# Control products ahead of a transpose fill, whole squares and a shorter affine in a gated channel sparsifier

## The chip, the cores and the metric

The kernel runs on one core of one Trainium2 chip. The metric is the device time of one execution in microseconds (us). The engines are PE (TensorE; its weight loads are shown as PEld), DVE (VectorE), ACT (ScalarE), POOL (GpSimd) and SP (SyncE, which only issues transfers here).

## What is computed

```python
# x: (32, 512, 56, 56) f32, W1, W3: (512, 512) f32
g = group_norm(x, groups=32, eps=1e-5)           # 16 channels a group
r = relu(g)
r = where(max_hw(r) - mean_hw(r) < 0.5, 0, r)    # per image and channel
bb = 1 - exp(-abs(max_c(r) - mean_c(r)))         # per image and pixel
y = bb * r
x_max, pooled = max_hw(y), mean_hw(y)
control1 = sigmoid(pooled @ W1.T)
control3 = relu(pooled @ W3.T); control3 = where(control3 < 1, 1.2, control3)
out = x + where(y < control1 * control3 * x_max, 0, y)
```

## The kernel before, in words

An image is four tiles (`t` = 0 to 3) of 128 channels x 3136 pixels, f32. Three images of x are kept in `xs`. Tiles 0 and 1 are worked on in place, tiles 2 and 3 in `rs`, so that their x is still there when POOL adds it back; x for tiles 0 and 1 is added by a transfer that accumulates (L787).

Each engine has one program written out by hand; the engines meet only at semaphores, and an engine's instructions run strictly in their order. One turn of the loop over images `s` on each engine holds work for three images: the end of image s-1, the middle of s and the start of s+1.

**ACT.** For image s+1 it squares every tile and sums along the pixels (`square_half`, L437 to L442, two halves of 1568 pixels a tile, written to `junk`, which nobody reads; L441 is the instruction). Each squaring waits until the one before it has been counted by `junk_step`. Between them stand, in the order of L513 to L522: the copy of the control rows of image s-1 out of PSUM (`copy_control`, L494) behind the first half of tile 2, the exponential for the sigmoid (`control_exp`, L498) behind the second half, the copy of the mean rows of image s (`copy_mean_rows`, L470) behind tile 0, that of the means (`copy_means`, L474) behind tile 1. The load order is tiles 2, 0, 1, 3. Then come the row means (`row_means`, L451 and L454), the first gate values (`gate_values`, L479 to L483: absolute value, exponential, 1 minus), the copy of the group's sums (`copy_group`, L459), and the four relus of image s+1 (L465, which applies the group norm as scale and bias), with gate values 1, 2, 3 between them, and then the pool sums of image s (`pool_sum`, L490): three for each tile, of 1536, 768 and 832 pixels, eleven of the twelve after the last relu.

**PE.** In the order of L396 to L428: transposes of image s (`turn`, L288, two blocks of 128 pixels of all four tiles, into one of two PSUM buffers; `turn` i waits until DVE has read buffer i-2), turns 0, 1, 2; the control products of image s-1 (`control_products`, L366: for each tile k, once its last pool sum is there, two matmuls of three columns x 512, in column groups 0 and 32 for even k, 64 and 96 for odd k); the control logits (L374); the mean rows of s (L298, 28 matmuls in four column groups); the sums over x of image s+1, two tiles (`sum_x`, L337); `turn_means` (L306); the other two tiles' sums; turns 3 and 4; the group's matmuls (`group_stats`, L348 for the means, L351 for the squares); `spread` 0 (L318, which puts the gate values into PSUM rows); turns 5 to 8, and so on with the other spreads. `keep_clock` (L325) issues matmuls that nobody reads.

**DVE.** The maxima over channels (`block_max`, L640, one for each turn), the differences (`differ`, L650), the gating with its maximum (`gate`, L657), and for image s-1, behind `block_max` 2, the control (L667 to L684) and the comparison with the threshold (`keep_tile`, L688). `differ` 0 stands between the third and fourth `keep_tile` and waits for the means from ACT.

**POOL.** For image s-1 the accumulating transfers of tiles 0 and 1 (L787), then the affine of image s+1 (`affine`, six small operations, L769 to L779), then the four additions of x for tiles 2 and 3 (L796). The relu of tile 3 waits for the last of these additions.

**SP.** Issues loads (L222) and stores (L232).

Of the kernel before, what the change touches and what calls it, by code (L numbers as in the profile page):

```python
# [4 lines left out]

F32 = mybir.dt.float32
BF16 = mybir.dt.bfloat16
I32 = mybir.dt.int32
ALU = mybir.AluOpType
ACT = mybir.ActivationFunctionType  # L10
# [2 lines left out]
P = 128  # L13
# [32 lines left out]
def gated_sparsifier(nc, x, w1, w3, out):  # L46
# [15 lines left out]
    GMAX = max(GPIX[g + 1] - GPIX[g] for g in range(NG))  # L62
    SUMS = ((0, 2), (2, 3), (3, 4))
    NS = len(SUMS)
    assert T == 4 and NBLK == 25 and LAST_W == 64 and NX * XCHUNK == HW and NM == 7 and GMAX == 832

    x_tiles = x.rearrange("b (t p) h w -> b p t (h w)", p=P)
# [2 lines left out]
    with ExitStack() as ctx:  # L70
        def sb(name, shape, dt=F32):
            return ctx.enter_context(nc.sbuf_tensor(name, shape, dt))
# [7 lines left out]
        xs = sb("xs", [P, XR, T, HW])  # L80
        rs = sb("rs", [P, 2, len(KEPT_X), HW])
        wt = sb("wt", [P, 2, T, C])
        junk = sb("junk", [P, HALF], BF16)
        rows = sb("rows", [P, C])
        control_sb = rows[:, :]
        mean_rows = rows[:, 0:MEAN_ROW]
# [9 lines left out]
        row_part = sb("row_part", [P, 2])  # L96
        ones = sb("ones", [P, 1])
        half_neg = sb("half_neg", [P, T])
        squares = sb("squares", [P, 2, T])
        row_sum = sb("row_sum", [P, 1])  # L100
        row_mean = sb("row_mean", [P, T])
        gst = sb("gst", [P, 2, T])
# [1 line left out]
        gvar = sb("gvar", [P, T])  # L104
        geps = sb("geps", [P, T])
        rstd = sb("rstd", [P, T])
        mrs = sb("mrs", [P, T])
        shift = sb("shift", [P, T])
        rsum = sb("rsum", [P, T])
        peak = sb("peak", [P, T])  # L110
# [91 lines left out]
        def half(tile, h):  # L202
            return tile[:, HALF * h:HALF * (h + 1)]
# [76 lines left out]
        def _(pe):  # L280
# [63 lines left out]
            def group_stats(s):  # L344
                pe.wait_ge(row_mean_ready, s + 1)
                if s > 1:
                    pe.wait_ge(logits_ready, s - 1)
                pe.matmul(ps_group[:, 0, :], group_pick[:, :], row_mean[:, :], start=True, stop=True)  # L348
                pe.wait_ge(squared, 2 * T * (s + 1))
                for h in range(2):  # L350
                    mm = pe.matmul(ps_group[:, 1, :], group_avg[:, :], squares[:, h, :], start=(h == 0),  # L351
                                   stop=(h == 1), skip_group_check=True)
                mm.then_inc(group_sums, 1)

            def count_fails(s):
# [2 lines left out]
                    mm = pe.matmul(ps_count, fails[:, t:t + 1], ones[:, :], start=(t == 0), stop=(t == T - 1))  # L358
                mm.then_inc(count_ready, 1)

            def control_products(s):
                for k in range(T):
                    pe.wait_ge(pooled_ready, NS * T * s + T * (NS - 1) + k + 1)
                    for m in range(2):
                        first = 32 * (m + 2 * (k % 2))
                        mm = pe.matmul(ps_control_rows[first:first + NS, :], pooled[:, k, :], wt[:, m, k, :],  # L366
                                       start=(k < 2), stop=(k >= T - 2), skip_group_check=True,
                                       tile_position=(0, first))
                mm.then_inc(control_rows, 1)

            def control_logits(s):
                pe.wait_ge(control_copied, s + 1)
# [22 lines left out]
            for s in range(B):  # L395
                pe.wait_ge(r_final, s + 1)  # L396
                turn(s, 0)
                turn(s, 1)
                turn(s, 2)
                if s > 0:  # L400
                    control_products(s - 1)
                    control_logits(s - 1)
                mean_rows_of(s)
                if s + 1 < B:
                    sum_x(s + 1, range(0, 2))
                turn_means(s)
                if s + 1 < B:
                    sum_x(s + 1, range(2, T))
                turn(s, 3)
                turn(s, 4)  # L410
                if s + 1 < B:
                    group_stats(s + 1)
                spread(s, 0)
                turn(s, 5)
                turn(s, 6)
                turn(s, 7)
                turn(s, 8)
                spread(s, 1)
                turn(s, 9)
                turn(s, 10)  # L420
                turn(s, 11)
                turn(s, 12)
                spread(s, 2)
                keep_clock(s, 3)
                spread(s, 3)
                if s + 1 < B:
                    count_fails(s + 1)
                    keep_clock(s, 2)  # L428
            control_products(B - 1)
            control_logits(B - 1)  # L430

        @block.scalar
        def _(act):
            steps = Steps(act, act_step)
            junk_step = Steps(act, squared)

            def square_half(s, n, h):  # L437
                t = LOAD_ORDER[n]
                act.wait_ge(x_loaded[s % XR][t][h], 16 * (s // XR + 1))
                junk_step.wait()  # L440
                junk_step.step(act.activation(junk[:, :], half(x_tile(s, t), h), ACT.Square,  # L441
                                              scale=float(HW) ** -0.5, accum_out=squares[:, h, t:t + 1]))  # L442

            def square_tile(s, n):
                for h in range(2):
                    square_half(s, n, h)

            def row_means(s):
                act.wait_ge(sx_summed, s + 1)
                junk_step.wait()  # L450
                steps.step(act.activation(junk[:, 0:XCHUNK], ps_rowsum, ACT.Identity,  # L451
                                          scale=1.0 / (PER_GROUP * HW), accum_out=row_sum[:, :]))
                steps.wait()
                act.activation(row_mean[:, :], row_tile[:, :], ACT.Identity, scale=row_sum[:, :]  # L454
                               ).then_inc(row_mean_ready, 1)
# [42 lines left out]
                act.activation(exp_neg[:, :], logits[:, 0:T], ACT.Exp, scale=-1.0).then_inc(exp_neg_ready, 1)  # L498

            act.wait_ge(consts_ready, 1)  # L500
            for n in range(T):
                square_tile(0, n)
            row_means(0)
            copy_group(0)
# [4 lines left out]
            for s in range(B):  # L509
                has_next = s + 1 < B  # L510
                if has_next:
                    square_half(s + 1, 0, 0)
                if s > 0:  # L513
                    copy_control(s - 1)
                if has_next:
                    square_half(s + 1, 0, 1)
                if s > 0:
                    control_exp(s - 1)
                if has_next:
                    square_tile(s + 1, 1)  # L520
                copy_mean_rows(s)
                if has_next:  # L522
                    square_tile(s + 1, 2)
                copy_means(s)
                if has_next:
                    square_tile(s + 1, 3)
                    row_means(s + 1)
                gate_values(s, 0)
                if has_next:
# [228 lines left out]
        def _(pool):  # L758
# [8 lines left out]
            def affine(s):  # L767
                pool.wait_ge(group_copied, s + 1)
                steps.step(pool.tensor_tensor(gsq[:, :], gst[:, 0, :], gst[:, 0, :], ALU.mult))  # L769
                steps.wait()  # L770
                steps.step(pool.tensor_tensor(gvar[:, :], gst[:, 1, :], gsq[:, :], ALU.subtract))
                steps.wait()
                steps.step(pool.tensor_scalar(geps[:, :], gvar[:, :], 0.0, GN_EPS, ALU.max, ALU.add))
                steps.wait()
                steps.step(pool.tensor_tensor(rstd[:, :], geps[:, :], half_neg[:, :], ALU.pow))  # L775
                steps.wait()
                steps.step(pool.tensor_tensor(mrs[:, :], gst[:, 0, :], rstd[:, :], ALU.mult))
                steps.wait()
                pool.tensor_scalar(shift[:, :], mrs[:, :], -1.0, 1.0, ALU.mult, ALU.mult).then_inc(affine_ready, 1)  # L779

            affine(0)
            for s in range(B):
# [35 lines left out]
```

## Time and profile before

| | |
|---|---|
| median of three runs | 1678.03 us (1676.78 to 1678.05) |
| the profiled execution: its time, its span | 1675.8 us, 1674.0 us |
| busy share | DVE 87%, PE 82%, ACT 81%, PEld 52%, POOL 36% |
| mean granted clock of PE | 0.942 of 2.4 GHz |
| DMA | 309 GB/s in the mean |

The span is the time from the first to the last instruction in the trace; the execution's own time is 1.8 us more, and the median of the runs 2.2 us above that. A busy share is an average over 32 images and tells how close an engine is to being full. It doesn't tell which waits set the time; for that stands the chain, which is followed back from the last instruction to what released it, step by step.

### The profile page before, as it was taken

The page shows a single profiled execution, that of the slowest core. Times are in us where ns is not written, and L with a number is a line of the kernel's source. Part 1 is how long each engine was busy: PE and PEld are TensorE (multiplying, and loading weights), DVE is VectorE, ACT ScalarE, POOL GpSimd, SP SyncE. Part 2 cuts the span into 40 slices and gives each one's busy share as a digit, 9 for nine tenths or more (in the row PEclk, how much of TensorE's full clock was granted, in tenths as well). Part 3 has the DMA queues.
Part 4 walks back from the last instruction along what each step waited for, and adds up shares of the span by engine and source line. Part 5 has one row for each costly group of instructions (what it writes and reads, how often), then busy time and mean ns, then how long its engine had stood idle before and what let it go on. Part 6 is the DMA issues. An engine that isn't in the chain of part 4 may idle for free.

```text
span 1674.0 us, 26770 instructions
## 1 busy us (share of the span) xinstructions
PE 1369.8 (82%) x10204; PEld 866.5 (52%) x10204; DVE 1459.4 (87%) x2192; ACT 1354.3 (81%) x2177; POOL 610.1 (36%) x446
## 2 busy tenths in 40 slices
PE   3889888888888988888888888888888888888761
PEld 1655455555455655455555555555545555545540
DVE  2598889988889988888998888988888998888996
ACT  7788888888888888888888888888888888888821
POOL 0042334442244443244443234443233444234440
PEclk8999999999999999999999999999999999999995
DMA  9259999999999999999999999999999999999973
GB/s 393 119 142 313 344 355 310 310 312 305 344 348 327 307 314 304 334 343 339 308 309 309 325 344 351 306 304 313 317 344 356 308 308 311 307 343 351 308 231 153
DMA packets 93348, 517.69 MB, mean 309 GB/s; under 512 B 10272, under 2 KB 10272, under 8 KB 93216
## 3 DMA queue, kind: packets, MB, share of 16 engines
q1 hardware_dynamic: 75360, 416.38, 61.7%
q0 software_dynamic: 17856, 99.56, 30.4%
q8 instruction: 81, 1.33, 0.3%
q14 instruction: 51, 0.42, 0.1%
HBM read 310.38 MB, written 205.52 MB: 308 GB/s over the span
## 4 chain that ended last, share of the span: by engine, by line
ACT 31%; PE 31%; POOL 29%; DVE 5%; issue 2%; DMA 1%; SPq 0%; DVEq 0%; ACTq 0%
POOL xs L796 25%; PE ps_gate L337 11%; ACT rs L490 11%; PE ps_gate L298 10%; ACT xs L490 9%; ACT rs L465 6%; PE ps_turn L288 4%; ACT junk L441 3%; PE ps_gate L374 2%; POOL rstd L775 2%; PE ps_gate L306 2%; DVE max_and_mean L640 1%; ACT rows L494 1%; PE ps_gate L351 1%; DMA xs<-in_x 1%
## 5 line engine op out<-in xcount | busy, mean ns | idle before, releaser
L640 DVE TENSOR_REDUCE max_and_mean<-ps_turn 128x2 f32<-128x1024 f32 x384 | 463.0, 1219 | 24.5 <-PE ps_turn L288 19.4
L288 PE MATMUL ps_turn<-ident,xs 128*128 128x128 f32 (+1 forms) x1600 | 329.5, 289 | 142.7 <-DVE max_and_mean L640 139.0
L796 POOL TENSOR_TENSOR xs<-xs,rs 128x1568 f32<-128x1568 f32 x124 | 433.3, 3528 | 0.9 <-DVE rs L688 0.9
L787 POOL DMA_DIRECT2D xs<-in_x x124 | 111.3, 966 | 877.9 <-DVE xs L688 780.8
L441 ACT ACTIVATE junk<-xs 128x1568 bf16<-128x1568 f32 x256 | 385.3, 1505 | 9.9 <-ACT junk L441 0.4
L288 PE MATMUL ps_turn<-ident,rs 128*128 128x128 f32 (+1 forms) x1600 | 315.9, 280 | 0.0
L288 PEld LDWEIGHTS ps_turn<-ident,xs 128*128 128x128 f32 (+1 forms) x1600 | 191.4, 144 | 239.5 <-DVE max_and_mean L640 184.5
L318 PE MATMUL ps_gate<-ident,bb 128*128 128x128 f32 (+1 forms) x1600 | 235.6, 301 | 62.4 <-ACT bb L483 61.5
L318 PEld LDWEIGHTS ps_gate<-ident,bb 128*128 128x128 f32 (+1 forms) x1600 | 215.3, 210 | 99.1 <-DVE ymax_parts L657 87.7
L465 ACT ACTIVATE xs<-xs,shift,rstd 128x3136 f32<-128x3136 f32 x64 | 192.1, 3001 | 85.8 <-POOL shift L779 80.5
L657 DVE CUSTOM_DVE_ANT_0 xs<-xs,ps_gate 128x768 f32<-128x768 f32 (+1 forms) x256 | 243.3, 959 | 10.4 <-PE ps_gate L318 8.6
L657 DVE CUSTOM_DVE_ANT_0 rs<-rs,ps_gate 128x768 f32<-128x768 f32 (+1 forms) x256 | 241.0, 961 | 7.5 <-issue 7.5
L465 ACT ACTIVATE rs<-xs,shift,rstd 128x3136 f32<-128x3136 f32 x64 | 192.1, 3002 | 60.5 <-POOL xs L796 60.5
L688 DVE SCALAR_TENSOR_TENSOR rs<-rs,thres 128x3136 f32<-128x3136 f32 x64 | 222.3, 3478 | 0.0
L688 DVE SCALAR_TENSOR_TENSOR xs<-xs,thres 128x3136 f32<-128x3136 f32 x64 | 220.3, 3483 | 1.1
L337 PE MATMUL ps_gate<-xs,sel 128*32 128x448 f32 x1792 | 205.9, 544 | 12.0 <-DMA xs<-in_x 12.0
L288 PEld LDWEIGHTS ps_turn<-ident,rs 128*128 128x128 f32 (+1 forms) x1600 | 206.3, 144 | 1.1
L490 ACT ACTIVATE xs<-xs 128x1536 f32<-128x1536 f32 (+2 forms) x192 | 203.2, 1059 | 1.2 <-DVE ymax_parts L657 1.2
L490 ACT ACTIVATE rs<-rs 128x1536 f32<-128x1536 f32 (+2 forms) x192 | 203.0, 1058 | 0.0
L325 PE MATMUL ps_turn<-wt,ident 128*128 128x512 f32 x316 | 171.5, 678 | 0.6
L337 PEld LDWEIGHTS ps_gate<-xs,sel 128*32 128x32 f32 x1792 | 62.7, 110 | 110.2 <-issue 109.6
L298 PE MATMUL ps_gate<-xs,chan_avg 128*32 128x512 f32 (+1 forms) x896 | 115.9, 542 | 0.0
(82 smaller groups left out, 1158.0 us busy)
## 6 DMA issues: line engine op xcount, KB each, us to landing
xs<-in_x SPq DMA_DIRECT2D x260, 784.0 KB, 13.8
out<-xs SPq DMA_DIRECT2D x256, 784.0 KB, 8.4
xs<-in_x POOLq DMA_DIRECT2D x124, 784.0 KB, 11.0
rs<-in_L_conv_W SPq DMA_DIRECT2D x2, 1024.0 KB, 17.2
```

The source lines that it names most:

```text
L288: mm = pe.transpose(ps_turn[0:w, n % 2, b - 2 * i, P * t:P * (t + 1)], r_tile(s, t)[:, P * b:P * b + w], ident[:, :])
L298: mm = pe.matmul(ps_mean_rows[32 * k:32 * k + 32, 0:w], chan_avg[:, 31 - j:63 - j], r_tile(s, t)[:, MEAN_ROW * j:MEAN_ROW * j + w], start= ...
L318: mm = pe.matmul(ps_gate[:, g % 2, first:first + w], bb[0:w, b:b + 1].to_broadcast([w, P]), ident[0:w, 0:w], start=True, stop=True)
L325: pe.matmul(ps_turn[:, NT * (s + 1) % 2, 0, :], ident[:, :], wt[:, 0, 0, :], start=True, stop=True, skip_group_check=True)
L337: mm = pe.matmul(ps_rowsum[32 * k:32 * k + 32, :], sel[:, t, :], x_tile(s, t)[:, XCHUNK * c:XCHUNK * (c + 1)], start=(q < 4), stop=(q >= N ...
L441: junk_step.step(act.activation(junk[:, :], half(x_tile(s, t), h), ACT.Square, scale=float(HW) ** -0.5, accum_out=squares[:, h, t:t + 1]))
L465: act.activation(r_tile(s, t), x_tile(s, t), ACT.Relu, bias=shift[:, t:t + 1], scale=rstd[:, t:t + 1], accum_out=rsum[:, t:t + 1]).then_in ...
L490: act.activation(y, y, ACT.Identity, accum_out=pooled[:, t, j:j + 1]).then_inc(pooled_ready, 1)
L640: ins = dve.tensor_reduce(max_and_mean[:, 2 * i:2 * i + 2, 0], ps_turn[:, n % 2, :, :], AX.X, ALU.max)
L657: dve.tensor_tensor_reduce(out=y, in0=y, in1=ps_gate[:, g % 2, 0:n], scale=1.0, scalar=0.0, op0=ALU.mult, op1=ALU.max, accum_out=ymax_part ...
L688: dve.scalar_tensor_tensor(r, r, thres[:, t:t + 1], r, ALU.is_ge, ALU.mult).then_inc(kept, 1)
L796: pool.tensor_tensor(o, o, half(r_tile(s - 1, t), h), ALU.add).then_inc(added, 1)
```

## The change

In words: on PE, `control_products` takes the tiles as an argument, and those of tiles 0 and 1 are issued ahead of turn 2, those of tiles 2 and 3 behind it; `group_stats` stands ahead of turn 4 and has three matmuls for the squares instead of two, two of them of one column. On ACT, the first tile to be squared is done in pieces of 784, 784 and 1568 pixels, every other tile in one instruction of 3136; the control copy stands behind the first piece, the exponential behind the second, the copy of the mean rows behind the third of the four tiles, and that of the means behind the fourth. `junk` is as many bytes as before, in 8-bit floats. The row means carry the minus sign, so that the affine is five operations and the last is the product.

```diff
-        junk = sb("junk", [P, HALF], BF16)
+        junk = sb("junk", [P, HW], FP8)
-        squares = sb("squares", [P, 2, T])
+        squares = sb("squares", [P, T + 2])
+    PIECES = ((0, HALF // 2), (HALF // 2, HALF), (HALF, HW))
...
-                pe.wait_ge(squared, 2 * T * (s + 1))
-                for h in range(2):
-                    mm = pe.matmul(ps_group[:, 1, :], group_avg[:, :], squares[:, h, :], start=(h == 0),
-                                   stop=(h == 1), skip_group_check=True)
+                pe.wait_ge(squared, (T + 2) * (s + 1))
+                first = LOAD_ORDER[0]
+                pe.matmul(ps_group[:, 1, :], group_avg[:, :], squares[:, 0:T], start=True, stop=False,
+                          skip_group_check=True)
+                for part in range(2):
+                    mm = pe.matmul(ps_group[:, 1, first:first + 1], group_avg[:, :],
+                                   squares[:, T + part:T + part + 1], start=False, stop=(part == 1),
+                                   skip_group_check=True)
...
                 turn(s, 1)
+                if s > 0:
+                    control_products(s - 1, range(0, 2))
                 turn(s, 2)
                 if s > 0:
-                    control_products(s - 1)
+                    control_products(s - 1, range(2, T))
                     control_logits(s - 1)
...
                 turn(s, 3)
-                turn(s, 4)
                 if s + 1 < B:
                     group_stats(s + 1)
+                turn(s, 4)
                 spread(s, 0)
...
+            def square(s, t, cols, part):
+                junk_step.wait()
+                junk_step.step(act.activation(junk[:, cols], x_tile(s, t)[:, cols], ACT.Square,
+                                              scale=float(HW) ** -0.5, accum_out=squares[:, part:part + 1],
+                                              saturate=False))
+
+            def square_piece(s, part):
+                t = LOAD_ORDER[0]
+                act.wait_ge(x_loaded[s % XR][t][part // 2], 16 * (s // XR + 1))
+                square(s, t, slice(*PIECES[part]), T + part if part < 2 else t)
...
+            def square_tile(s, n):
                 t = LOAD_ORDER[n]
+                wait_loaded(act, s, t)
+                square(s, t, slice(0, HW), t)
...
-                                          scale=1.0 / (PER_GROUP * HW), accum_out=row_sum[:, :]))
+                                          scale=-1.0 / (PER_GROUP * HW), accum_out=row_sum[:, :],
+                                          saturate=False))
...
                 if has_next:
-                    square_half(s + 1, 0, 0)
+                    square_piece(s + 1, 0)
                 if s > 0:
                     copy_control(s - 1)
                 if has_next:
-                    square_half(s + 1, 0, 1)
+                    square_piece(s + 1, 1)
                 if s > 0:
                     control_exp(s - 1)
                 if has_next:
+                    square_piece(s + 1, 2)
                     square_tile(s + 1, 1)
+                    square_tile(s + 1, 2)
                 copy_mean_rows(s)
                 if has_next:
-                    square_tile(s + 1, 2)
+                    square_tile(s + 1, 3)
                 copy_means(s)
                 if has_next:
-                    square_tile(s + 1, 3)
                     row_means(s + 1)
...
-                steps.step(pool.tensor_tensor(mrs[:, :], gst[:, 0, :], rstd[:, :], ALU.mult))
-                steps.wait()
-                pool.tensor_scalar(shift[:, :], mrs[:, :], -1.0, 1.0, ALU.mult, ALU.mult).then_inc(affine_ready, 1)
+                pool.tensor_tensor(shift[:, :], gst[:, 0, :], rstd[:, :], ALU.mult).then_inc(affine_ready, 1)
```

## Rows read from the trace of the kernel before

**Rows 1.** The page, part 4: the chain that ended last, by engine.
```profile
ACT 31%; PE 31%; POOL 29%; DVE 5%; issue 2%; DMA 1%; SPq 0%; DVEq 0%; ACTq 0%
```

**Rows 2.** The chain in order of time: start us, us, what; group copies of two images.
```profile
111.45 0.19 ACT gst L459
...
1557.15 0.19 ACT gst L459
```

**Rows 3.** The waits from 115 to 1560: us in total, times, longest us.
```profile
DVE logits L667 <- PE ps_gate L374: 105.4, 29, 4.3
```

**Rows 4.** Windows: us, busy (instructions) of PE, PEld, DVE, ACT, POOL; clock, DMA share, GB/s.
```profile
745.00:750.00 5.00, 5.00 (x60) 2.20 (x56) 4.89 (x8) 3.23 (x5) 0.36 (x1) 1.00 0.74 307
...
785.00:790.00 5.00, 4.57 (x21) 3.19 (x21) 3.65 (x7) 5.00 (x13) 0.00 (x0) 0.67 1.02 396
```

**Rows 5.** The chain in order of time, one period.
```profile
743.49 1.05 PE ps_gate L374 x8
...
749.94 2.99 PE ps_gate L337 x28
...
757.05 1.90 PE ps_turn L288 x16
...
759.55 0.19 ACT gst L459
...
762.09 0.20 POOL shift L779
762.29 13.95 POOL xs L796 x4
```

**Rows 6.** The timeline of ACT: start us, us, instruction [idle before it <- releaser].
```profile
729.48 0.19 ACT L479 ACTIVATE absd<-diff 128x7 f32<-128x7 f32 x1
...
731.61 1.47 ACT L490 ACTIVATE rs<-rs 128x1536 f32<-128x1536 f32 x1
...
734.55 0.83 ACT L490 ACTIVATE xs<-xs 128x768 f32<-128x768 f32 x1
...
741.37 1.49 ACT L441 ACTIVATE junk<-xs 128x1568 bf16<-128x1568 f32 x1
...
742.86 0.57 ACT L494 ACTIVATE rows<-ps_gate 128x512 f32<-128x512 f32 x1
...
744.83 0.19 ACT L498 ACTIVATE exp_neg<-logits 128x4 f32<-128x4 f32 x1
...
746.71 1.51 ACT L441 ACTIVATE junk<-xs 128x1568 bf16<-128x1568 f32 x1
...
750.00 0.60 ACT L470 ACTIVATE rows<-ps_gate 128x512 f32<-128x512 f32 x1 [1.68 <-PE ps_gate L298]
...
757.42 0.54 ACT L451 ACTIVATE junk<-ps_gate 128x448 bf16<-128x448 f32 x1
```

**Rows 7.** The timeline of PE and its weight loads, around the control products.
```profile
737.93 0.44 PE L288 MATMUL ps_turn<-ident,xs 128*128 128x128 f32 x2 [1.47 <-DVE max_and_mean L640]
...
738.95 3.59 PE L366 MATMUL ps_gate<-wt,pooled 128*3 128x512 f32 x16
...
1587.25 0.11 PEld L366 LDWEIGHTS ps_gate<-wt,pooled 128*3 128x3 f32 x8 [0.17 <-ACT xs L490]
...
1588.07 0.13 PEld L366 LDWEIGHTS ps_gate<-wt,pooled 128*3 128x3 f32 x4 [0.71 <-ACT rs L490]
```

**Rows 8.** The timeline of ACT at the start of the run.
```profile
20.26 0.54 ACT L451 ACTIVATE junk<-ps_gate 128x448 bf16<-128x448 f32 x1 [0.26 <-PE ps_gate L337]
...
22.15 0.18 ACT L459 ACTIVATE gst<-ps_gate 128x8 f32<-128x8 f32 x1 [0.92 <-PE ps_gate L351]
```

**Rows 9.** The timeline of DVE.
```profile
712.08 1.23 DVE L640 TENSOR_REDUCE max_and_mean<-ps_turn 128x2 f32<-128x1024 f32 x1 [0.20 <-PE ps_turn L288]
...
727.87 0.15 DVE L650 TENSOR_REDUCE diff<-max_and_mean 128x7 f32<-128x14 f32 x1
...
736.66 3.62 DVE L640 TENSOR_REDUCE max_and_mean<-ps_turn 128x2 f32<-128x1024 f32 x3
```

More of the change, by code:

```diff
@@ L6 @@
 F32 = mybir.dt.float32
-BF16 = mybir.dt.bfloat16
+FP8 = mybir.dt.float8e4
 I32 = mybir.dt.int32
@@ L106, in gated_sparsifier @@
         rstd = sb("rstd", [P, T])
-        mrs = sb("mrs", [P, T])
         shift = sb("shift", [P, T])
@@ L359, in count_fails, with control_products @@
                 mm.then_inc(count_ready, 1)
-            def control_products(s):
-                for k in range(T):
+            def control_products(s, products):
+                for k in products:
                     pe.wait_ge(pooled_ready, NS * T * s + T * (NS - 1) + k + 1)
@@ L368, in control_products @@
                                        tile_position=(0, first))
-                mm.then_inc(control_rows, 1)
+                if k == T - 1:
+                    mm.then_inc(control_rows, 1)
             def control_logits(s):
@@ L428, in _ @@
                     keep_clock(s, 2)
-            control_products(B - 1)
+            control_products(B - 1, range(T))
             control_logits(B - 1)
@@ L435, in _ @@
             junk_step = Steps(act, squared)
-            def square_half(s, n, h):
-                t = LOAD_ORDER[n]
[L439 to L446, printed above, removed]
+            def square(s, t, cols, part):
[8 more added lines that the diff above has]
+            def square_tile(s, n):
+                t = LOAD_ORDER[n]
+                wait_loaded(act, s, t)
+                square(s, t, slice(0, HW), t)
             def row_means(s):
@@ L500, in _ @@
             act.wait_ge(consts_ready, 1)
-            for n in range(T):
+            for part in range(3):
+                square_piece(0, part)
+            for n in range(1, T):
                 square_tile(0, n)
```

## The prediction

> **What bounds the kernel now.** The page came first. DVE has the highest busy share (table above), but the chain that ended last is shared by ACT, PE and POOL, about 30% each, with DVE at 5% [rows 1]. So no engine's throughput sets the time; a ring through three engines does. The start of the group copy (`gst`, L459) of the third image and of the last one are 1445.70 us and 29 images apart: 49.85 us a period [rows 2]. The waits say how much room DVE has beside the ring: it stands idle 105.4 us in 29 images, 3.6 each, until the control logits come [rows 3]. The DMA engines have less: they are full most of a period, yet between 745 and 750 the share is 0.74, some 1.3 us free of 5 [rows 4], and loads are issued two images ahead, so a gain of up to about a microsecond a period meets no transfer.
>
> The chain in order of time, for one period, is what the sum rests on [rows 5]. I count from c, the start of the control copy on ACT (L494, 742.86 [rows 6]). Then: logits on PE until 743.49 + 1.05 = 744.54 = c+1.68, mean rows until 749.94 (5.40), the first two tiles' sums 2.99 (c+10.07), the turned means and the other two tiles' sums until 757.05 (c+14.19), turns 3 and 4, 1.90, the group matmuls, `gst` at 759.55 = c+16.69, the affine operations until 762.29, four additions on POOL 13.95, then the last relu and 15 us of ACT work up to the next c.
>
> **The change part by part.**
>
> (a) *Affine, five operations for six.* The sign moves into the scale of L451. The removed L779 is 0.20 in every period's chain (762.09 to the adds at 762.29, [rows 5]), and the hand-over ahead of it is some 0.07 (an estimate, from the 0.06 between PE and ACT in (b)). Nothing covers it, so it is all gain: **0.27**.
>
> (b) *First squares in three pieces.* Today ACT ends its last pool sum at 741.37, runs a half (1.49) and copies the control rows at 742.86 [rows 6]. A piece of 784 costs less: 1536 columns take 1.47, 768 take 0.83 [rows 6], so 0.833 ns a column and 0.84 for 784. ACT would be free at 742.21. But the 16 product records of PE end at 738.95 + 3.59 = 742.54 [rows 7], and a hand-over is 0.06 (mean rows end at 749.94, ACT starts at 750.00 [rows 5, 6]). So the copy could start at 742.60, not 742.21: gain 0.26 of the 0.65 that ACT saves.
>
> (c) *Two tiles' products ahead of turn 2.* Two tiles that are ready together run at the same time: eight weight loads (two tiles of two matmuls in two passes) at 1587.25, the third tile's four at 1588.07 [rows 7], so 0.82 for a pair. A single tile takes as long. The products follow the last pool sums, 832 columns and so 0.88 apart. Counted back from 741.37 with the read-back behind each, tile 0 is ready just before its products start at 738.95, tile 1 at 739.7, and tile 1's products leave the array at about 740.6. Only then come eight transposes, at 1.90/16 = 0.12 each [rows 5] 0.95, and some 0.2 to change over (the products' loads at 1587.25 come 0.17 after the last transpose's [rows 7]). Tiles 2 and 3 then start together at about 741.7 instead of 741.5 for tile 3 today. The copy comes at about 742.76. Of the 0.26 of (b), **0.10** is left; bounds 0 and 0.26. I take 0.10. Today turn 2 stands ahead of all products and holds nothing up, since its wait for DVE ends at 737.93 [rows 7], before tile 0 is ready. DVE gets turn 2's fill some 2.7 later, out of its idle 3.6.
>
> (d) *Other squares whole, and tile 2's ahead of the mean rows' copy.* The exponential needs the logits, DVE's copy of them and two hand-overs, some 0.27 (an estimate: the 0.15 of a small DVE operation at 727.87 [rows 9] and twice 0.06): c+1.95; today c+1.97, behind the second half [rows 6]. So the third piece starts at c+2.14. Halves follow each other at 1.69 (746.71 - 744.83 less 0.19 [rows 6]); a whole tile adds 1568 x 0.833 = 1.31, so 3.00. Tile one starts at c+3.83, tile two at c+6.83 and ends its write 2.82 later (1.51 + 1.31) at c+9.65; the copy (0.60, [rows 6]) ends at c+10.25. PE wants it at c+10.07. Today ACT idles 1.68 before that copy [rows 6]; the change turns this cover into a **wait of 0.2** on PE, and queued behind it are the means and two tiles' sums, hence everything. The sums end at c+14.4. Against it: two read-backs and waits fewer, 0.4 of ACT, which only pays later: `row_means` starts with the sums at c+14.45, where today it starts 0.37 after them (757.42 against 757.05 [rows 5, 6]).
> The Trainium skill, "Perfetto Trace Analysis", section "Optimizing Scalar/DVE Operations", speaks against this part: where ScalarE isn't saturated but makes others wait, breaking instructions up may let work complete sooner. By that rule the whole squares are the wrong way round here, and halves with the copy between them would give back the 0.2 a period, some 6 us in all; the trace agrees that the copy waits for nothing but PE today.
>
> (e) *Group matmuls ahead of turn 4.* From L451 to `gst` startup shows 22.15 - 20.26 = 1.89, with no transposes in between [rows 8]; today it takes 759.55 - 757.42 = 2.13 [rows 5, 6]. One matmul more (three for two, each in two passes) is 0.24, two of the logits' eight records in 1.05 (an estimate, at 0.12 each, [rows 5]). So c+14.45+1.89+0.24 = c+16.58 against c+16.69: **0.11**; bounds 0.05 (the waits add up) and 0.35 (the copy of (d) in time). Turn 4 is now behind a wait. DVE runs turn 3's maxima first, until about c+17.8, and turn 4 is filled at c+17.6. The late one is turn 5, behind spread 0: DVE waits for it even today, 0.20 at 712.08 [rows 9]; it comes 0.95 - 0.11 = 0.8 later, and DVE is late by that from there on. ACT wants the difference of the last group 1.46 after it is there (727.87 + 0.15 = 728.02, and 729.48 [rows 6, 9]). With ACT 0.4 earlier and DVE 0.8 later some 0.2 is left: just hidden. The last pool sum starts at 740.5, 4 us after DVE's last gate (its next maxima start at 736.66 [rows 9]). DVE's room falls from 3.6 to about 2.4.
>
> (f) *8-bit output.* No row shows one. f32 out is 0.833 ns a column, and bf16 out (1568 in 1.49) lies on the same line [rows 6]. Below nothing isn't excluded by that, but two widths on one line leave no width term: taken at nothing. Upper bound: as much again for the halved width, which is the slower rival.
>
> **Sum.** 0.27 + 0.10 + 0.11 = 0.48 a period, over 29 periods 13.9 us. At the start the last square has to wait for its tile's second half, as today, but is then 1.31 longer. It holds `row_means`, which starts on ACT at 20.26 today [rows 8], the group matmuls and, behind them on PE, the turning of the weights, which releases relu 0: with the extra matmul 1.5 us lost, and nothing hides it. The first image and the last two lie outside the 29 periods and give back about 0.5 (an operation less in each, products that come earlier). So -12.9 on the profiled execution's own 1675.8 (span 1674.0): 1662.9. The median of the runs is 2.2 above that execution: **1665**. The measurement can tell 0.2% (3.4 us) from no change.
>
> **Rivals.**
> *The covers hold better.* Products cost nothing (0.16 more) and the mean rows' copy is in time (0.2 more), if whole squares save more than I count. Then 0.84 a period, 24.4 us less 1.0: 1655. For: both places miss by 0.2 or less. Against: both are worked out from dense rows. 0.18.
> *The gain turns into waits.* DVE is later by over 0.2 more than I have it, and the last gate values wait for it; or PE restarts slowly after each new wait. Each 0.1 costs 3 us; 0.4 leaves 0.1 a period: 1676. For: three margins of 0.2 in one ring. 0.16.
> *Slower: the 8-bit output.* Place: between c+2.14 and c+9.65 ACT writes 7840 squared columns with no idle time, ahead of a copy that PE waits for. Every 1% on them is 0.065 a period. It decides from 0.45/6.53 = 7%, 0.89 ns a column. At 25% it is +1.6 - 0.5 = 1.1 a period: 1711. Against: the width made no difference so far. 0.10. The Trainium skill, "ScalarE: Activation LUTs", section "What ACT_TABLE_LOAD costs", gives 186 ns + 0.833 per column with immediates, for fp32 and bf16; it names no 8-bit type. By that figure (an estimate) a whole tile is 2.80, and the trace agrees, 1.49 for 1568.
> *PE's clock.* From 785 to 790 the granted clock was 0.67 [rows 4], 3 us before the products' end at the next c; today such stretches lie beside DVE's gates and cost no period anything. The change gives PE one more idle stretch before turn 2. If the low level reached logits and mean rows in one image of five (5.4 + 1 us doubled), that is six times 6.4: 1703. The Trainium skill, "TensorE: Matmul & The Clock Gate", says that the gate follows how busy the engine has been lately and knows two levels. 0.06.
> Forecast: 0.50.
>
> **How the numbers follow.** The range takes in forecast, the upside and the eaten gain, 0.84: 1653 to 1680. Faster by over 0.2% (below 1674.7) is forecast, upside and a small part of the waits: 0.71. Same 0.13, slower 0.16.
>
> **What would show it.** Period 49.3 to 49.4 by `gst`. ACT idle about 0.5 before the control copy, waiting for L366. A square of 3136 at 2.82, of 784 at 0.84. PE idle about 0.2 before L306, on the mean rows' copy. ACT no longer idle before that copy. From L451 to `gst` 2.1. POOL from `gst` to the adds 0.27 shorter. DVE idle 1 to 1.5 before turn 2's maxima. The first relu 1.5 later. The forecast is wrong if squares aren't on the 0.833 line, if ACT idles before L479, or if the low clock reaches the stretch from c to c+16.

## The result and the profile after

The changed kernel takes 1668.03 us (median of four runs, 1666.36 to 1668.34) against 1678.04: a ratio of 0.9939, 95% interval 0.9927 to 0.9951. It is 10 us faster; 13 were forecast. The profiled execution took 1667.76 us, its span 1666.0; the two profiled executions are 8.0 us apart, where 12.9 were forecast for them. The medians lie further apart because the profiled execution before was 2.2 us under its median and this one 0.3.

The page of the changed kernel, part 1 and the engines' shares of the chain [rows 1]:

```profile
span 1666.0 us, 26674 instructions
...
PE 1362.0 (82%) x10268; PEld 873.6 (52%) x10268; DVE 1458.8 (88%) x2192; ACT 1339.7 (80%) x2049; POOL 604.2 (36%) x414
...
ACT 39%; POOL 29%; PE 23%; DVE 5%; issue 3%; DMA 1%; SPq 0%; ACTq 0%; DVEq 0%
```

ACT's share of the chain rose from 31 to 39% and PE's fell from 31 to 23%, while POOL's stayed. The ring is the same; the stretch beside the mean rows has moved from PE to ACT. The timeline of ACT shows it, for one period with c = 740.38 (the control copy, here L507; L483 is the mean rows' copy, L463 the first step of the row means, L472 the group copy, `gst`):

```profile
114.07 0.18 ACT L472 ACTIVATE gst<-ps_gate 128x8 f32<-128x8 f32 x1 [0.47 <-PE ps_gate L354]
...
740.38 0.60 ACT L507 ACTIVATE rows<-ps_gate 128x512 f32<-128x512 f32 x1 [0.55 <-PE ps_gate L370]
740.87 0.85 ACT L446 ACTIVATE junk<-xs 128x784 fp8e4<-128x784 f32 x1
742.32 0.21 ACT L511 ACTIVATE exp_neg<-logits 128x4 f32<-128x4 f32 x1 [0.51 <-DVE logits L683]
742.43 1.49 ACT L446 ACTIVATE junk<-xs 128x1568 fp8e4<-128x1568 f32 x1
744.13 2.82 ACT L446 ACTIVATE junk<-xs 128x3136 fp8e4<-128x3136 f32 x1
747.15 2.82 ACT L446 ACTIVATE junk<-xs 128x3136 fp8e4<-128x3136 f32 x1
749.97 0.58 ACT L483 ACTIVATE rows<-ps_gate 128x512 f32<-128x512 f32 x1
...
754.84 0.54 ACT L463 ACTIVATE junk<-ps_gate 128x448 fp8e4<-128x448 f32 x1 [1.38 <-PE ps_gate L337]
...
756.95 0.18 ACT L472 ACTIVATE gst<-ps_gate 128x8 f32<-128x8 f32 x1 [0.47 <-PE ps_gate L354]
...
1547.79 0.18 ACT L472 ACTIVATE gst<-ps_gate 128x8 f32<-128x8 f32 x1 [0.47 <-PE ps_gate L354]
```

Read it against [rows 2, 6]. The period is (1547.79 - 114.07)/29 = 49.44 us, and 49.42 in all but two of them (49.72 and 49.54), against 49.85. The copy that used to idle 1.68 for the mean rows now has no idle time before it and starts at c+9.59: ACT is late, not PE. The group copy is at c+16.57 (forecast 16.58, before 16.69). A square of 3136 takes 2.82 with an 8-bit output, as the 0.833 ns a column of the prediction say. ACT idles 0.55 before the control copy and 0.51 before the exponential, so most of what the pieces save is spent waiting.

The timeline of DVE, at the end of the same image, [rows 9] before:

```profile
784.53 2.35 DVE L656 TENSOR_REDUCE max_and_mean<-ps_turn 128x2 f32<-128x1024 f32 x2
788.79 1.22 DVE L656 TENSOR_REDUCE max_and_mean<-ps_turn 128x2 f32<-128x1024 f32 x1 [1.92 <-PE ps_turn L288]
791.54 0.17 DVE L683 COPY logits<-ps_gate 128x8 f32<-128x8 f32 x1 [1.52 <-PE ps_gate L379]
```

DVE's spare time before the logits was 3.6 us a period in one piece [rows 3]; now it is two pieces, 1.92 before turn 2's maxima and 1.52 before the logits. The waits from 115 to 1550 add a third, before turn 5's maxima; both kinds of maxima together are 73.9/29 = 2.5 a period:

```profile
DVE max_and_mean L656 <- PE ps_turn L288: 73.9, 58, 2.1
DVE logits L683 <- PE ps_gate L379: 44.0, 29, 1.5
```

The balance in spans: 29 periods gave 12.0 us. At the start `gst` of the first image is 2.26 later (22.15, [rows 8], against 24.41). 0.9 of that is that the last load landed later (the last square starts at 19.30 instead of 18.40; in run e4 below, whose squares are those of before, it is 19.09, so this varies without the change). 1.36 is the longer last square and the added matmul. The next two images add 0.36, and the last image lost 1.4. This is the timeline of PE in it, the changed kernel's first and the old kernel's after it:

```profile
1594.88 1.79 PE L318 MATMUL ps_gate<-ident,bb 128*128 128x128 f32 x12 [3.54 <-ACT bb L496]
1598.50 0.69 PE L288 MATMUL ps_turn<-ident,xs 128*128 128x128 f32 x2 [1.83 <-DVE max_and_mean L656]
1598.98 0.64 PE L288 MATMUL ps_turn<-ident,rs 128*128 128x128 f32 x2
...
1603.50 0.44 PE L288 MATMUL ps_turn<-ident,xs 128*128 128x128 f32 x2
```

```profile
1604.24 2.90 PE L318 MATMUL ps_gate<-ident,bb 128*128 128x128 f32 x12 [3.54 <-ACT bb L483]
1607.86 0.44 PE L288 MATMUL ps_turn<-ident,xs 128*128 128x128 f32 x2 [0.72 <-DVE max_and_mean L640]
1608.14 0.38 PE L288 MATMUL ps_turn<-ident,rs 128*128 128x128 f32 x2
...
1611.60 0.44 PE L288 MATMUL ps_turn<-ident,xs 128*128 128x128 f32 x2 [0.24 <-DVE max_and_mean L640]
```

Both idle 3.54 us before the spread. Before, the low clock fell on the spread (2.90), which nobody awaits there; after, on the next turns, which DVE awaits. Counted from the last group copy, both kernels start the first of these turns at 50.71; three turns later the changed kernel is behind by 1.26. Whether the change moved the low clock there, or only this execution had it there, is not shown: there is one profile of each. 12.0 - 2.6 - 1.4 = 8.0 is the difference of the spans.

### The profile page after: what moved, and what is told of

Read it like the earlier page. It is cut to its first block, busy times and chain, and to the rows that moved or that the text cites. A ratio compares the mean times of both kernels' runs of the same rounds, so it can differ in the third digit from the quotient of the medians.

```text
span 1666.0 us, 26674 instructions
## 1 busy us (share of the span) xinstructions
PE 1362.0 (82%) x10268; PEld 873.6 (52%) x10268; DVE 1458.8 (88%) x2192; ACT 1339.7 (80%) x2049; POOL 604.2 (36%) x414
## 4 chain that ended last, share of the span: by engine, by line
ACT 39%; POOL 29%; PE 23%; DVE 5%; issue 3%; DMA 1%; SPq 0%; ACTq 0%; DVEq 0%
POOL xs L810 25%; ACT junk L446 14%; ACT rs L503 8%; ACT xs L503 8%; PE ps_gate L337 6%; ACT rs L478 6%; PE ps_gate L370 6%; PE ps_turn L288 4%; PE ps_gate L379 2%; PE ps_gate L306 2%; POOL rstd L791 2%; ACT rows L507 1%; ACT rows L483 1%; PE ps_gate L354 1%; DMA xs<-in_x 1%
## 5 line engine op out<-in xcount | busy, mean ns | idle before, releaser
L446 ACT ACTIVATE junk<-xs 128x784 fp8e4<-128x784 f32 (+2 forms) x192 | 372.0, 1938 | 10.2 <-DMA xs<-in_x 2.5
L288 PE MATMUL ps_turn<-ident,rs 128*128 128x128 f32 (+1 forms) x1600 | 321.3, 284 | 0.0
L288 PEld LDWEIGHTS ps_turn<-ident,xs 128*128 128x128 f32 (+1 forms) x1600 | 194.9, 146 | 235.0 <-DVE max_and_mean L656 190.6
L318 PE MATMUL ps_gate<-ident,bb 128*128 128x128 f32 (+1 forms) x1600 | 231.0, 299 | 10.5 <-ACT bb L496 10.5
L318 PEld LDWEIGHTS ps_gate<-ident,bb 128*128 128x128 f32 (+1 forms) x1600 | 219.6, 213 | 35.4 <-DVE ymax_parts L673 20.6
L325 PE MATMUL ps_turn<-wt,ident 128*128 128x512 f32 x316 | 155.0, 622 | 0.2
L370 PE MATMUL ps_gate<-wt,pooled 128*3 128x512 f32 x512 | 95.7, 605 | 47.4 <-ACT xs L503 47.4
```

Of the source, the lines that this page charges most:

```text
L288: mm = pe.transpose(ps_turn[0:w, n % 2, b - 2 * i, P * t:P * (t + 1)], r_tile(s, t)[:, P * b:P * b + w], ident[:, :])
L318: mm = pe.matmul(ps_gate[:, g % 2, first:first + w], bb[0:w, b:b + 1].to_broadcast([w, P]), ident[0:w, 0:w], start=True, stop=True)
L325: pe.matmul(ps_turn[:, NT * (s + 1) % 2, 0, :], ident[:, :], wt[:, 0, 0, :], start=True, stop=True, skip_group_check=True)
L446: junk_step.step(act.activation(junk[:, cols], x_tile(s, t)[:, cols], ACT.Square, scale=float(HW) ** -0.5, accum_out=squares[:, part:part ...
```

## The experiments

Each ratio is to the kernel before, timed beside the run (its medians were 1677.8 to 1678.2). The period is that of the group copies of images 2 to 31, as above; the place of `gst` is the median of these images.

| run | median us | ratio, 95% interval | period us | `gst`, us behind c |
|---|---|---|---|---|
| kernel before | 1678 | | 49.85 | 16.69 |
| changed kernel | 1668.0 | 0.9939 (0.9927 to 0.9951) | 49.44 | 16.56 |
| e1_products_behind | 1659.8 | 0.9897 (0.9880 to 0.9914) | 49.21 | 16.56 |
| e2_mean_rows_early | 1679.8 | 1.001 (1.000 to 1.0019) | 49.83 | 16.37 |
| e3_turn4_first | 1718.9 | 1.0245 (1.0228 to 1.0262) | 51.12 | 17.13 |
| e4_five_alone | 1668.2 | 0.9944 (0.9927 to 0.9960) | 49.55 | 16.69 |
| e5_differ_late | 1693.5 | 1.0097 (1.0080 to 1.0114) | 50.20 | 17.37 |
| e6_three_mended | 1685.6 | 1.0045 (1.0028 to 1.0061) | 49.94 | 17.38 |
| e7_turn4_clock | 1684.5 | 1.0043 (1.0026 to 1.0060) | 49.99 | 17.13 |
| e8_squares_first | 1683.9 | 1.0036 (1.0022 to 1.0051) | 49.94 | 17.37 |
| e9_copies_as_before | 1661.3 | 0.9898 (0.9882 to 0.9915) | 49.22 | 16.37 |
| e10_products_and_copies | **1654.2** | 0.9861 (0.9844 to 0.9877) | 48.97 | 16.37 |
| e11_squares_first_again | 1658.6 | 0.9888 (0.9872 to 0.9905) | 49.07 | 15.80 |
| e12_first_tile_halves | 1657.9 | 0.9880 (0.9864 to 0.9896) | 49.15 | 16.12 |

### One part alone: the affine

```diff
 # the kernel before, with the diff's edits to affine() and to the scale in row_means(), nothing else
```

> The kernel before with the affine in five operations and the sign in the row means' scale, nothing else. Theory: the removed operation and its hand-over are on the ring of every image and nothing covers them: a period of 49.57 to 49.58 instead of 49.85, 8.7 us less than before over 31 images, 1669: two thirds of the ring's gain come from this part. Rival: ACT or POOL finds another wait in its place (the additions wait for the fourth comparison, the relu for a late difference), and less than 0.1 is left: 1675 or more.

49.55 and 1668.2 us. The theory said 49.57 and 1669. The removed operation and its hand-over are worth 0.30 a period, and by themselves as much as the whole change. Everything else in it gives another 0.11 a period, 3.2 us in 29, and loses 2.4 of them again at the start and in the last image (spans 1666.8 and 1666.0). This run's last image, too, is 1.0 longer than that of the kernel before, so most of the 1.4 lost there does not hang on the other parts of the change.

### Undoing the split of the products

```diff
                 turn(s, 1)
-                if s > 0:
-                    control_products(s - 1, range(0, 2))
                 turn(s, 2)
                 if s > 0:
-                    control_products(s - 1, range(2, T))
+                    control_products(s - 1, range(T))
```

> The changed kernel with all four tiles' control products behind turn 2 again. Theory: the split costs what the pieces save. In the changed kernel tiles 2 and 3 start on the array 0.27 us after tile 3 is ready, because eight transposes stand before them. Without the split tile 3 should start 0.05 after it is ready and the control copy 1.22 after the last pool sum instead of 1.48: a period of 49.17 to 49.20 instead of 49.42, and 7 us less in all, 1661. Rival: DVE is 0.8 later beside ACT than in the kernel before, turn 2 waits for its maxima, and with all products behind turn 2 they all come later: a period of 49.42 or more, 1668 or more.

8 us faster than the changed kernel, at 49.16 in most periods (a few are 0.1 to 0.3 longer). The control copy comes 1.22 after the last pool sum, as the theory said. The two timelines of PE, first the changed kernel and then this run:

```profile
785.83 1.91 PE L370 MATMUL ps_gate<-wt,pooled 128*3 128x512 f32 x8 [1.44 <-ACT xs L503]
787.66 0.44 PE L288 MATMUL ps_turn<-ident,xs 128*128 128x128 f32 x2
...
788.69 1.04 PE L370 MATMUL ps_gate<-wt,pooled 128*3 128x512 f32 x8
```

```profile
734.13 2.70 PE L370 MATMUL ps_gate<-wt,pooled 128*3 128x512 f32 x16
```

With the split, tiles 2 and 3 start at 788.69, although tile 3 has been ready since 788.41; the copy comes 1.48 after the last pool sum, where halves had it at 1.49. So the split ate nearly all of the 0.26 that the pieces bring without it.

### Turn 4 and the group matmuls

```diff
                 turn(s, 3)
+                turn(s, 4)
                 if s + 1 < B:
                     group_stats(s + 1)
-                turn(s, 4)
```

> The changed kernel with turn 4 ahead of the group matmuls again. Theory: the row means are ready at c+15.4, 0.1 after turn 3 is issued; with turn 4 first the group matmuls start at c+16.2 and their copy comes at c+17.1 instead of c+16.57: a period of 49.95 to 50.0, 1684, slower than the kernel before, because the added matmul stays. Rival: DVE's lateness (turn 5 is filled 0.8 late) costs as much as the order wins, and putting turn 4 first changes the period by less than 0.2: 1668 to 1674.

The group copy came at c+17.13, as expected, but the period was 51.2 instead of 50.0. The third and fourth period of this run were 49.98 and 49.97; from the fifth on they stood near 51.2. The windows and the timeline of PE around the products of one image:

```profile
755.00:757.50 2.50, 0.31 (x2) 0.10 (x4) 2.41 (x3) 2.50 (x7) 0.00 (x0) 0.95 1.02 401
757.50:760.00 2.50, 2.50 (x9) 0.22 (x6) 0.00 (x0) 2.50 (x7) 0.00 (x0) 0.50 1.01 416
```

```profile
757.19 2.75 PE L370 MATMUL ps_gate<-wt,pooled 128*3 128x512 f32 x8 [2.27 <-ACT xs L503]
759.88 0.69 PE L288 MATMUL ps_turn<-ident,xs 128*128 128x128 f32 x2
```

PE had been idle for 2.27 us (1.44 in the changed kernel), the granted clock stood at its lower level, 1.2 GHz, and the products of tiles 0 and 1 took 2.75 instead of 1.91, and turn 2 in the chain 1.37 instead of 1.02: 1.2 us together, on the ring. But the length of the idle stretch alone does not settle it. This is the product row of the last period before the fall:

```profile
194.96 1.91 PE L370 MATMUL ps_gate<-wt,pooled 128*3 128x512 f32 x8 [2.26 <-ACT xs L503]
```

Here PE idled as long, and the products still took 1.91. The next run fills the idle stretch with one more of the matmuls that nobody reads:

```diff
                     count_fails(s + 1)
-                    keep_clock(s, 2)
+                    keep_clock(s, 3)
```

> The kernel with turn 4 ahead of the group matmuls, with three instead of two of the matmuls that nobody reads ahead of the next image's turn 0. There PE was idle for 2.3 us after turn 1, the granted clock stood at 0.5 from there until 3.8 us later in every period from the fifth on, and products and turn 2 took 2.75 and 1.37 instead of 1.91 and 1.02. Theory: of the 1.8 a period that turn 4 costs, 0.55 is the group copy and 1.2 is this low clock; with one more matmul the idle stretch is about 1.4, as in the changed kernel, the clock stays, and the period is 49.97 to 50.0 as in the first periods of that run: 1685. Rival: the clock follows the load of the whole period or the low stretch only moves: 51.1 or more, 1718.

49.99 and 1684.5: the 1.2 is gone. So the place of turn 4 is worth 0.55 a period by its order (49.99 against 49.44), and 1.2 more was the clock. The Trainium skill, "TensorE: Matmul & The Clock Gate", section "What's actually happening", says that the clock follows how busy the engine has been and knows two levels; the trace agrees, 0.50 beside 1.00.

### The copy of the mean rows, and what POOL waits for

```diff
                     square_tile(s + 1, 1)
-                    square_tile(s + 1, 2)
                 copy_mean_rows(s)
                 if has_next:
+                    square_tile(s + 1, 2)
                     square_tile(s + 1, 3)
                 copy_means(s)
```

> The changed kernel with the mean rows' copy one square earlier on ACT, between the second and the third tile. Theory: PE's wait on that copy ahead of the turned means is on the ring; without it they start at c+10.0 instead of c+10.2, and the group copy comes 0.2 earlier: a period of 49.2, 6 us less, 1662. Rival: what PE gains there it loses in waiting for the row means, since ACT is the bound in that stretch: 49.42, 1668.

Neither. The group copy came 0.2 earlier behind c, as the theory said, and the kernel was 12 us slower than the changed one. The timelines of POOL and of DVE in this run:

```profile
711.52 0.79 POOL L785 TENSOR_TENSOR gsq<-gst 128x4 f32<-128x4 f32 x1 [0.83 <-ACT gst L472]
712.39 0.20 POOL L787 TENSOR_TENSOR gvar<-gst,gsq 128x4 f32<-128x4 f32 x1
```

```profile
708.70 0.17 DVE L666 TENSOR_REDUCE diff<-max_and_mean 128x6 f32<-128x12 f32 x1 [0.62 <-ACT max_and_mean L487]
708.78 3.48 DVE L704 SCALAR_TENSOR_TENSOR rs<-rs,thres 128x3136 f32<-128x3136 f32 x1
```

An operation on four columns takes 0.79 on POOL instead of 0.20, and ends 0.05 after DVE's fourth comparison (712.26). That comparison was 0.6 late because the difference ahead of it waits for the means, whose copy still stood behind the fourth square. The first attempt to take this apart moved the difference:

```diff
 # DVE, on top of e2
-                differ(s, 0)
                 if s > 0:
                     keep_tile(s - 1, KEEP_ORDER[3])
+                differ(s, 0)
```

> The kernel with the mean rows' copy one square earlier, and on DVE the first difference (which waits for the means) behind the fourth comparison instead of ahead of it. There POOL's first affine operation took 0.79 us instead of 0.20, from c+16.63 to c+17.42, and DVE's fourth comparison ended at c+17.36, 0.6 later than in the changed kernel, since the difference ahead of it waited for the means. Theory: POOL's two-input operation does not go forward while DVE's two-input comparison runs. With the difference behind it the comparison ends at about c+16.65, the POOL operation is back at 0.20, and the 0.2 won at the group copy is kept: a period of 49.2, 1662. Rival: the POOL operation is slow for another reason (transfers, the earlier place in time): it stays at 0.8 and the period at 49.8, 1679.

POOL's operation was back at 0.19, but `gst` fell to c+17.37 and the run to 1693. The waits of ACT show why:

```profile
ACT absd L492 <- DVE diff L666: 42.4, 29, 1.5
```

The gate values stand ahead of the group copy on ACT, and wait for that difference. I had moved a step past one queue without looking who waits for it on the next. Two runs built on the same edit were spoiled by it, at c+17.38 and c+17.37. They say nothing of POOL's wait, and both missed their forecasts (1653 to 1660, and periods of 48.5 to 48.9) by far; e6 still shows the products' gain, 49.94 against e5's 50.20.

```diff
 # e6: e5 with all products behind turn 2
 # e8: e6 with the squares' group matmuls ahead of the wait for the row means and of turn 3, spread(s, 0) behind turn 5
```

> The one before with all control products behind turn 2 as well. Theory: the two gains lie one behind the other on the ring and add up, 0.25 for the products and 0.2 for the copy: a period of 48.95 to 49.0, 1653 to 1655. Rival: DVE comes late for the last gate values (it had about 0.4 of margin there in the changed kernel) and takes 0.1 to 0.2 of it back: 49.1 to 49.15, 1658 to 1660.

> The three-times mended kernel with the squares' group matmuls ahead of the wait for the row means and ahead of turn 3, and spread 0 behind turn 5. The group copy should come at about c+15.9 instead of c+16.37. Theory of the shared path: DVE's fourth comparison still ends at c+16.6, POOL's first affine operation starts at c+16.15 and is stretched until then, to about 0.5, and only 0.1 to 0.2 of the 0.5 is kept: a period of 48.8 to 48.9. Rival: POOL and DVE don't get in each other's way: the operation takes 0.20 and the period is 48.5.

The clean form leaves DVE alone and puts both copies where the kernel before has them:

```diff
                     square_tile(s + 1, 1)
-                    square_tile(s + 1, 2)
                 copy_mean_rows(s)
                 if has_next:
-                    square_tile(s + 1, 3)
+                    square_tile(s + 1, 2)
                 copy_means(s)
                 if has_next:
+                    square_tile(s + 1, 3)
                     row_means(s + 1)
```

> The changed kernel with both copies (mean rows, means) where the kernel before has them, each one square earlier; DVE's order untouched. Theory: the mean rows' copy waits only for PE and the means' copy is in time for DVE, so the fourth comparison ends at c+16.65, the group copy comes at c+16.37, POOL's first affine operation starts at c+16.63 and takes 0.20: a period of 49.2 to 49.25, 1662 to 1663. Rival: the third square now runs into the mean rows' wait, ACT comes late with the row means and the group copy stays at c+16.56 or later: 49.42 or more, 1668.

49.22 and 1661.3, as the theory had it: `gst` at c+16.37, POOL's first operation at c+16.63 with 0.19, the comparison's end at c+16.65. With the products as well:

```diff
 # e10: e9 and e1 together
```

> The one before with all control products behind turn 2. Theory: both gains add up, 0.25 and 0.2 a period: 48.95 to 49.0, 1653 to 1655. Rival: DVE comes late for the last gate values and takes part of it back: 49.1, 1658.

48.97 and 1654.2: the two gains add up, and this beats both kernels, by 24 us and by 14. Its waits, DVE from 115 to 1550:

```profile
DVE logits L681 <- PE ps_gate L379: 89.2, 29, 3.2
DVE max_and_mean L654 <- PE ps_turn L288: 17.9, 30, 0.6
```

DVE still has 89.2/29 = 3.1 us a period before the logits, so it had nothing to take back.

Then POOL's wait by itself, in steps of how early the group copy is:

```diff
 # e11: e10, with in group_stats: the three squares' matmuls first, then wait row_mean_ready and the matmul
 # for the means; and on PE: group_stats, turns 3, 4, 5, spread(s, 0)
 # e12: e1, with the first tile in halves (PIECES = ((0, HALF), (HALF, HW))) and one group matmul fewer
```

> The one before with the squares' group matmuls ahead of the wait for the row means and ahead of turn 3, and spread 0 behind turn 5: the group copy comes at about c+15.9, 0.7 ahead of the end of DVE's fourth comparison (c+16.65). Theory: POOL's two-input operation does not go forward until that comparison has ended; the first affine operation starts at c+16.15 and takes about 0.5, and only 0.1 of the 0.5 is kept: 48.85 to 48.9, 1650 to 1652. Rival: the two do not get in each other's way, the operation takes 0.20: 48.5, 1641.

> The changed kernel with all products behind turn 2 and the first tile in two halves instead of three pieces (one group matmul fewer). The control copy is back at 1.49 after the last pool sum, 0.26 later than with pieces and products behind. Against it ACT saves its two idle stretches beside the copy and the exponential: the second half fills the wait for the logits, the mean rows' copy is in time, and the group copy could come at about c+16.15. Theory: POOL's affine cannot start before DVE's fourth comparison ends at c+16.65, so of these 0.4 only 0.2 counts: a period of 49.2 to 49.25. If POOL is not held: 49.0. Rival: the pieces are worth their 0.26 in full and halves give 49.43.

POOL's first operation in e11:

```profile
750.33 0.67 POOL L783 TENSOR_TENSOR gsq<-gst 128x4 f32<-128x4 f32 x1 [0.96 <-ACT gst L470]
751.07 0.20 POOL L785 TENSOR_TENSOR gvar<-gst,gsq 128x4 f32<-128x4 f32 x1
```

and DVE's comparison beside it, which ends at 750.94:

```profile
747.47 3.47 DVE L702 SCALAR_TENSOR_TENSOR rs<-rs,thres 128x3136 f32<-128x3136 f32 x1
```

The start of POOL's operation moved with the group copy, its end did not follow: c+16.04 to 16.71 in e11, 16.38 to 16.68 in e12, 16.63 to 16.82 in e9, 16.63 to 17.42 in e2, with the comparison ending at 16.65, 16.62, 16.65 and 17.36. So where POOL's operation starts well inside the comparison, it ends 0.04 to 0.07 behind the comparison's end, in all 30 images from the third on of e2, e11 and e12; where the comparison is over or within 0.04 of its end, as in e9, it takes its own 0.19. The engines' programs meet only at semaphores, but here is a meeting that no semaphore names. The Trainium skill, "SBUF — State Buffer", section "Who interferes with whom", says that a VectorE instruction with two SBUF inputs contends with a GpSimd instruction that reads SBUF, for a shared read interface; the trace agrees with these four, though it shows the wait and not the interface. Of the 0.57 by which e11's group copy is earlier than e10's, 0.11 is left at the end of that operation. The hold came as forecast, the time did not: 49.07 and 1658.6 against 48.85 to 48.9 and 1650 to 1652. The period is even 0.10 longer than e10's, because its chain now runs through DVE. Turn 5 can't be filled before turn 3's maxima are read, spread 0 now stands behind turn 5, and DVE then waits for turn 6. Whether e11 would pass e10 with another order of the turns was not tried.

e12 is the surprise among the runs that beat the change: two halves and no pieces, 49.15. Its control copy is later than e1's, but ACT has no second idle stretch and the group copy is at c+16.12. The forecast of 49.20 to 49.25 was close; that the pieces' 0.26 is mostly what ACT then idles away is my reading of it. POOL's operation is held here too, 0.30 instead of 0.19.

## Why the prediction was right, and where not

The sign, the range and the size hold: 10 us gained, 13 forecast. Part of that closeness is luck. The working was for the profiled executions, and there 8.0 were gained of 12.9: the 29 periods gave 12.0 for 13.9, and what lies outside them cost 4.0 where 1.0 was counted. By its own steps:

(a) *Affine*: 0.27 forecast, 0.30 by e4 alone. Right, and it is the gain.

(b), (c) *Pieces and split*: 0.10 forecast, 0.01 measured (1.48 against 1.49 after the last pool sum), inside the bounds of 0 and 0.26. Mis-sized, by 0.04 each, are the start of tiles 2 and 3, 0.37 after the last pool sum (788.69 and 788.32) where I had 0.33, and the way from there to the copy, 1.10 instead of 1.06. For the change from products to transposes I had no row; that it makes the first of the two is not shown by itself. That the split itself costs 0.2 is shown by e1.

(d) *Copy of the mean rows behind two whole squares*: a wait of 0.2 forecast; e9 gives 0.22 a period back. So the price set beside the rule of the Trainium skill ("Perfetto Trace Analysis", section "Optimizing Scalar/DVE Operations"), 6 us, was right: e9 gains 6.8. But e9 mends the wait with whole squares, by the place of the copies alone; halves there were not tried, so no run tests that rule.

(e) *Group matmuls ahead of turn 4*: 0.11 forecast, 0.13 measured (16.56 from 16.69). DVE's lateness was hidden, as forecast: ACT waits 0.27 for it before one pool sum, and the relu behind that sum waits for POOL anyway. Its room did not shrink to 2.4: 1.5 is left before the logits and 2.5 before the maxima. The gain of the order alone, 0.55, is shown by e7; the added matmul was not taken out by itself.

(f) *8-bit output*: no cost, 2.82 on the 0.833 line; the slower rival fell by that row.

*The start and the end*: 1.5 forecast for the start, 1.36 measured, and 0.9 more from the late load; 0.5 were to come back in the first image and the last two, and instead the next two images cost 0.36 and the last 1.4. *The clock*: it did not reach the ring's PE stretch in the 29 periods, but 1.26 of the 1.4 in the last image came with the low level on the turns, which I had not counted. e3 shows that the mechanism of that rival is real, at 1.2 us a period with 0.8 us more of idle time.

The three terms of the ring as measured, 0.30, 0.01 and 0.13, make 0.44; the period fell by 0.41 in the mean and by 0.43 where it is 49.42.

Missing from the prediction was POOL's wait for DVE. It cost the change next to nothing, since POOL's first operation started at c+16.83, 0.08 after the comparison ended at c+16.75. In one image it was held, at 0.32 instead of 0.20, and the period that follows is the one of 49.54. That is luck: with the group copy much over 0.1 earlier, the sum's rule that what is gained there is gained on the ring would have been wrong.

## What to carry to other kernels

When a ring through several engines sets the time, follow one period from one fixed point and write each step's place beside it; the sum of the moves then comes out to a few hundredths. Before counting a step as gained, look who holds what the next engine needs: here a four-column operation on POOL waited for a comparison on DVE that no semaphore names. And when a step is moved behind another, name everyone who waits for it, also at second hand.

## What was not expected of the hardware

A small POOL operation that reads SBUF starts in the trace and stands until DVE's two-input comparison has ended: 0.79, 0.67 and 0.30 us instead of 0.20. PE's clock stood at its lower level during the products from the fifth period of e3 on, where PE had idled 2.3 us before them, and they took 2.75 us instead of 1.91; with 1.4 us of idle time (the changed kernel, e7) it never did so in these periods. One period of e3 with 2.26 us of idle time kept the full clock, so what else decides is open. An 8-bit output costs ACT the same as the wider ones: 1.51 us for 1568 columns, as with bf16, 2.82 for 3136 and 0.85 for 784.
